# A two-layer transformer kernel on one core: projections in place of products of zeros in the first rounds, and the routing's exponential behind the first scores copy

## The chip, the cores and the metric

The kernel runs on one core of a Trainium2 chip. The metric is device time in microseconds (us) for one execution of the whole program; lower is better. Engines: PE (TensorE, matrix products), DVE (VectorE), ACT (ScalarE), POOL (GpSimd) and SP (SyncE, which issues most DMAs).

## The reference, cut to what matters

The input x has 32 sequences of 256 tokens with 128 channels, 8192 tokens in all, in float32. There are two layers of the same shape: a layer norm, an attention over the normalised tokens, a mixture of experts over the same normalised tokens whose silu is a gate, and `x = x + s * g`. Layer 0, cut to the part that the change touches:

```python
xn = _layernorm(x)                                  # per token, 128 channels
q1, k1, q2, k2 = rotary(xn @ Wq1.T), ...            # 16 heads of 8
v = xn @ Wv.T
s1, s2 = q1 @ k1.T, q2 @ k2.T                       # per head, 256 x 256
y = (causal(s1 / 8 * s2 / 8) @ v) @ Wout.T
scores = sigmoid(xn @ gate_w + bias)                # 8 experts, the best two are taken
w = top_2(scores) / (sum + 1e-6)
```

No softmax stands in layer 0: the pattern is the product of two score matrices. Layer 1 has a softmax attention and experts with a capacity; the change doesn't touch it.

## The kernel before, in words

Every engine has a program of its own, written out by hand, and they meet at semaphores. The order of instructions in each program is the order of execution. The stages are: eight rounds of the first layer norm (about the first 65 us), the loop of layer 0's attention (192 units and a tail), layer 0's experts, a stage that ends layer 0 and normalises again, and layer 1 in a loop of 32 blocks with its experts in the middle.

**The rounds.** The 64 tiles of 128 tokens go through in eight rounds of eight tiles (k = 0 to 7). For each round DVE takes the statistics (lines 1119 to 1125, called one round ahead), POOL raises the variance to the power -0.5 (line 624), DVE makes the shift and normalises three of the eight tiles (line 1130), and ACT normalises the other five (line 843). PE turns the eight tiles with transposes into two banks of PSUM (line 1752), ACT copies these to the turned tokens `XT` (line 851), and PE multiplies them with the 8 columns of the gate (line 1760, 8 products per round, each recorded as two). ACT scales round k + 1 before it copies round k. Between the transposes and the gate's products PE has to wait for ACT's copies; there `products_of_zeros` (line 1736) puts three products of 128x128 zeros with 128x512 zeros, whose result nobody reads. Twenty more of them stand ahead of round 0. In round 7 a projection stands in that place in the kernel before already.

**Projections and rotations of block 0.** A block is one sequence, two tiles. `projection(b, x)` (lines 1438 and 1439) makes query or key x of block b twice, as it is and with swapped halves, into PSUM bank 7, and DVE's `rotate(b, x)` (lines 1142 and 1147) turns it with cosines and sines. There is one such bank, so each projection waits for the rotation of the one before. In the kernel before, projections 0, 1 and 2 of block 0 stand behind the gate's products of rounds 2, 3 and 4, the values (line 1445) behind those of round 5, projection 3 in round 7. DVE's program has rotations 0, 1 and 2 in its own rounds 5, 6 and 7: rotation 0 stands ahead of the statistics of round 7, rotation 1 behind the normalising of round 6, rotation 2 behind that of round 7.

**The head of the loop.** PE's unit u = -1 makes the first kind of scores for unit 0 (line 1470) and projection 1 of block 1. Unit 0 makes the first scores for unit 1 and the second for unit 0; it waits for ACT's copy of the first scores of unit 0 (`first_scores_copy`, line 720). ACT has the exponential of the gate's sigmoid (line 854) ahead of that copy, and it waits for DVE's addition of the bias (line 1060, semaphore `gate`), which is the first step of the generator `gate_first`. DVE takes that step at u = -1, behind rotations 0 and 1 of block 1.

The lines that matter:

```python
        if k == 7:
            projection(e, m, s, 0, 3)
        else:
            products_of_zeros(e, m, 3)
        e.wait_ge(s.xt, 2 * k + 2)
```

Of the kernel before, what the change touches and what calls it, by code (L numbers as in the profile page):

```python
# [9 lines left out]
ACT = mybir.ActivationFunctionType  # L10
# [39 lines left out]
def route_step(u):  # L50

    if u < 25:
        return 1 if u == -1 else 2 if u % 6 in (1, 3) else 0
    if u < 61:
        return {25: 1, 27: 1, 31: 1, 33: 1, 37: 2, 39: 1, 45: 1, 49: 2, 51: 1}.get(u, 0)
    return 1 if u % 6 in (1, 3) else 0
# [772 lines left out]
def scalar_program(e, m, s):  # L829
    a = m.a  # L830
    for dst, src in ((m.ident[:], a["c_ident"]), (m.small[:], a["c_small"]), (m.wgA[:, 0, :], a["g0"]),
                     (m.wgA[:, 1, :], a["g1"]), (m.bias8[:], a["bias"].partition_broadcast(P)),
                     (m.scl[:], a["us"].partition_broadcast(P))):
        e.dma_start(dst, src).then_inc(s.const, 16)
    e.wait_ge(s.const, 96)
    e.copy(m.identb[:], m.ident[:])
    e.dma_start(m.upb[:], a["up_b"].rearrange("e (p j) -> p e j", j=4)).then_inc(s.upb, 16)
    route_consts(e, m, s, m.r0)
    for k in range(9):
        if k < 8:  # L840
            e.wait_ge(s.nb, k + 1)
            for i in range(8 * k, 8 * k + 5):
                ins = e.activation(m.XN[:, i, :], m.XN[:, i, :], ACT.Identity, bias=m.nb[:, i:i + 1], scale=m.rstd[:, i:i + 1])
            ins.then_inc(s.norm_a, 1)
        if k == 8:
            value_copy(e, m, s, 0)
            query_masks(e, m, s, 0, 0, range(4))
        for g in (2 * k - 2, 2 * k - 1):
            if k >= 1:
                e.wait_ge(s.xpose, g + 1)  # L850
                e.copy(m.XT[:, g * 512:g * 512 + 512], m.PS[g % 2][:]).then_inc(s.xt, 1)
    query_masks(e, m, s, 0, 1, range(4))
    e.wait_ge(s.gate, 1)
    e.activation(m.SC[:], m.SC[:], ACT.Exp, scale=-1.0).then_inc(s.gate_exp, 1)
    for u in range(-1, NU + 4):
        v, b = u % 6, u // 6
        if v == 2 and u >= 0:
            if b + 1 < NB:
                value_copy(e, m, s, b + 1)
        if u + 1 < NU:  # L860
            first_scores_copy(e, m, s, u + 1)
        if u < 0:
            continue
        if b + 1 < NB:
            if v in (0, 1):
                query_masks(e, m, s, b + 1, 0, (2 * v, 2 * v + 1))
            if v in (3, 4):
                query_masks(e, m, s, b + 1, 1, (2 * v - 6, 2 * v - 5))
        if v == 2 and b >= 1:
            e.wait_ge(s.pv, 3 * b)  # L870
            e.copy(m.RS[:, (b - 1) * 256:b * 256], m.PS[6][:, 0:256]).then_inc(s.yt, 1)

    expert_act(e, m, s, m.x0, 0, ACT.Gelu, lambda i, j: m.UB[:, i, j:j + 1])

    e.wait_ge(s.sw, 80)
    shared_act(e, m, s, 0)
    for g in range(NG + 5):
        if 0 <= g - 5 < NG:
            end_act(e, m, s, g - 5, 1)
        if g in (NG + 1, NG + 2):  # L880
            queries_copy(e, m, s, g - NG)
        if g + 1 < NG:
            shared_act(e, m, s, g + 1)
        if g == NG + 3:
            queries_apart(e, m, s, 0, range(4))
            maximum_copy(e, m, s, 0)
        if 0 <= g - 5 < NG - 1:
            end_act(e, m, s, g - 5, 2)
        if 0 <= g - 1 < NG:
            end_act(e, m, s, g - 1, 0)  # L890
        if g == NG - 1:
            queries_copy(e, m, s, 0)
            keys_copy(e, m, s, 0)
        if g == NG:
            e.activation(m.scl[:, 1:2], m.scl[:, 0:1], ACT.Exp, scale=-1.0).then_inc(s.scl_a, 1)
            keys_apart(e, m, s, 0)
            value_pad(e, m, s, 0)
        if g == NG + 1:
            keys_copy(e, m, s, 1)
        if g == NG + 2:  # L900
            keys_apart(e, m, s, 1)
    e.wait_ge(s.scl, 1)
    for t in range(NB + 1):
        if t == 1:
            e.wait_ge(s.gate, 2)
            e.activation(m.LG[:], m.LG[:], ACT.Exp).then_inc(s.gate_exp, 1)
        if t < NB:
            exponents(e, m, s, t, 0)
        if t == 0:
            end_act(e, m, s, NG - 1, 2)  # L910
        if t + 2 < NB:
            keys_copy(e, m, s, t + 2)
            keys_apart(e, m, s, t + 2)
        if t + 1 < NB:
            value_pad(e, m, s, t + 1)
        for p in pairs_combined(t):
            e.wait_ge(s.fcomb, p + 1)
            if p >= NF:
                e.wait_ge(s.fex, p - NF + 1)
            e.activation(m.ZE[p % NF], m.ZU[p % NF], ACT.Tanh, scale=0.5).then_inc(s.ftanh, 1)  # L920
        if t + 1 < NB:
            queries_apart(e, m, s, t + 1, (0, 1))
        if t < NB:
            exponents(e, m, s, t, 1)
        if t + 1 < NB:
            queries_apart(e, m, s, t + 1, (2, 3))
            maximum_copy(e, m, s, t + 1)
        if t + 3 < NB:
            queries_copy(e, m, s, t + 3)
        if t == MOE_AFTER:  # L930
            expert_act(e, m, s, m.x1, 1, ACT.Relu, lambda i, j: m.b1s[:, i // 8, j:j + 1])
# [203 lines left out]
def rotate(e, m, s, b, x):  # L1135

    i, rt = 4 * b + x, m.RT[x % 2]
    e.wait_ge(s.proj, i + 1)
    e.wait_ge(s.w0, 32)
    if x % 2 == 0 and i >= 2:  # L1140
        e.wait_ge(s.rq, 2 * b + x // 2)
    e.tensor_tensor(rt[:], m.PS[7], m.cs[:], ALU.mult).then_inc(s.rt, 1)
    if x % 2 == 1:
        if b >= 2:
            e.wait_ge((s.sc1, s.sc2)[x // 2], 6 * (b - 1))
        e.wait_ge(s.rt, i + 1)
        e.tensor_tensor(m.KK[b % 2][:, x // 2, :], rt[:, 0:256], rt[:, 256:512], ALU.add).then_inc(s.ka, 1)
# [154 lines left out]
def vector_program(e, m, s):  # L1302
# [10 lines left out]
    for k in range(8):  # L1313
# [6 lines left out]
        if k in (5, 6, 7):  # L1320
            rotate(e, m, s, 0, k - 5)
    rotate(e, m, s, 0, 3)
    rotate(e, m, s, 1, 0)
    rotate(e, m, s, 1, 1)

    gate = gate_first(e, m, s, o)
    for u in range(-1, NU + 4):
        v, b = u % 6, u // 6
        if 0 <= u < NU:
# [95 lines left out]
def projection(e, m, s, b, x):  # L1425
    e.wait_ge(s.w0, 32)
    if x == 3:
        e.wait_ge(s.vm, b + 1)
    elif 4 * b + x >= 1:
        e.wait_ge(s.rt, 4 * b + x)  # L1430
    if x == 0 and b == ROUTED_BY[0]:
        e.wait_ge(s.cnt_row, 1)
    if x == 0 and b == ROUTED_BY[1]:
        e.wait_ge(s.total_sb, 1)
    if x == 0 and b in ROUTED_BY[2:]:
        e.wait_ge(s.low_used, ROUTED_BY.index(b) - 1)
    xt = m.XT[:, b * 256:b * 256 + 256]
    e.matmul(m.PS[7][:, 0:256], m.W0[:, 2 * x, :], xt, start=True, stop=True)
    e.matmul(m.PS[7][:, 256:512], m.W0[:, 2 * x + 1, :], xt, start=True, stop=True).then_inc(s.proj, 1)

def values(e, m, s, b):
    e.wait_ge(s.rt, 4 * b + 3)
    for c in range(2):
        i = e.matmul(m.PS[7][:, c * P:(c + 1) * P], m.XT[:, b * 256 + c * P:b * 256 + (c + 1) * P], m.W0[:, 8, :],
                     start=True, stop=True)
    i.then_inc(s.vproj, 1)
# [285 lines left out]
def products_of_zeros(e, m, n):  # L1733

    for _ in range(n):
        e.matmul(m.PS[5], m.zero[:, 0:P], m.zero[:, 0:512], start=True, stop=True)

def tensor_program(e, m, s):
    PS = m.PS  # L1740
    e.wait_ge(s.zero_ready, 1)
    products_of_zeros(e, m, 20)
    e.wait_ge(s.const, 96)
    for k in range(8):
        e.wait_ge(s.norm, k + 1)
        e.wait_ge(s.norm_a, k + 1)
        for q in range(2):
            g = 2 * k + q
            if g >= 2:
                e.wait_ge(s.xt, g - 1)  # L1750
            for j in range(4):
                i = e.transpose(PS[q][:, j * P:(j + 1) * P], m.XN[:, 4 * g + j, :], m.ident[:])
            i.then_inc(s.xpose, 1)
        if k == 7:
            projection(e, m, s, 0, 3)
        else:
            products_of_zeros(e, m, 3)
        e.wait_ge(s.xt, 2 * k + 2)
        for t in range(8 * k, 8 * k + 8):
            i = e.matmul(PS[6][:, t * E:(t + 1) * E], m.XT[:, t * P:(t + 1) * P], m.wgA[:, 0, :], start=True, stop=True)  # L1760
        if k == 7:
            i.then_inc(s.logits, 1)
        if k in (2, 3, 4):
            projection(e, m, s, 0, k - 2)
        if k == 5:
            values(e, m, s, 0)
    projection(e, m, s, 1, 0)

    for u in range(-1, NU + 4):
# [224 lines left out]
```

## Time and profile before

| what | value |
|---|---|
| median of 3 runs | 1807.51 us (1805.01 to 1809.03) |
| profiled execution, its time | 1808.82 us |
| its span, first to last instruction | 1807.6 us |
| mean granted TensorE clock over the span | 0.985 |
| PE busy | 1685.4 us, 93% of the span |
| DVE, ACT, POOL busy | 1011.3, 988.9, 769.6 us |

In rows of a timeline the first number is the start in us from the span's start, the second the length, then engine, line, operation, out<-in, shapes and the count of records; a float32 product has two records. In brackets stands the idle time ahead and what ended it. The end of a matrix product is modelled and overlaps the next, so differences of starts are the better measure.

### The profile page before, as it was taken

What the parts mean: (1) busy time and instruction counts of PE and PEld (TensorE: products, weight loads), DVE (VectorE), ACT (ScalarE), POOL (GpSimd) and SP (SyncE); (2) the same over time, 40 slices, a digit from 0 to 9 for tenths busy, and PEclk for the clock granted to TensorE, in tenths of its full rate; (3) what the DMA queues carried; (4) which work ended last, traced back from release to release, by engine and by line L of the source; (5) the groups of instructions that cost most, each with busy time, mean ns of one, the idle gap of its engine ahead of it and who ended that gap; (6) DMA issues with size and microseconds to landing.
All of it is one profiled execution on the core that took longest, in us unless ns stands there. A gap on an engine that the chain in (4) does not pass through costs nothing. (4 is left out here: it accounts for less than half of the span.)

```text
span 1807.6 us, 49638 instructions
## 1 busy us (share of the span) xinstructions
PE 1685.4 (93%) x19554; PEld 1200.3 (66%) x19554; DVE 1011.3 (56%) x2111; ACT 988.9 (55%) x1803; POOL 769.6 (43%) x828
## 2 busy tenths in 40 slices
PE   9899999999998999999999689999998999989996
PEld 5544444444445999988777456666657999976664
DVE  5488788777774222221899576454452222238886
ACT  3565666666665444444454455666654444446674
POOL 4133477777773454444012103555543555540000
PEclk9999999999999999999999799999999999999999
DMA  9900001100002777775343100111112233323331
GB/s 337 374 1 2 5 26 56 64 25 28 28 27 86 222 220 225 229 210 150 114 139 105 50 2 20 37 34 37 36 33 72 85 95 87 94 79 96 96 96 43
DMA packets 172276, 170.17 MB, mean 94 GB/s; under 512 B 20272, under 2 KB 139440, under 8 KB 169104
## 3 DMA queue, kind: packets, MB, share of 16 engines
q1 hardware_dynamic: 151296, 128.83, 23.7%
q0 software_dynamic: 16832, 34.64, 5.6%
q10 hardware_dynamic: 3920, 3.53, 0.7%
q8 instruction: 159, 2.61, 0.6%
q14 instruction: 69, 0.57, 0.1%
HBM read 97.29 MB, written 69.63 MB: 92 GB/s over the span
## 5 line engine op out<-in xcount | busy, mean ns | idle before, releaser
L550 POOL DMA_INDIRECT xd<-s_XN,s_slots x256 | 250.2, 977 | 157.9 <-issue 94.4
L720 ACT ACTIVATE s_S<-ps 128x1024 f32<-128x1024 f32 x192 | 196.7, 1024 | 187.5 <-PE ps L1470 183.5
L1337 DVE TENSOR_TENSOR s_PP<-ps,s_S 128x1024 f32<-128x1024 f32 x192 | 234.8, 1223 | 105.2 <-PE ps L1470 76.6
L1470 PE MATMUL ps<-s_QM,s_KK 32*128 32x512 f32 x1536 | 220.8, 640 | 29.5 <-issue 28.7
L784 ACT ACTIVATE s_PX<-ps,s_scl 128x1024 f32<-128x1024 f32 x128 | 135.6, 1110 | 185.7 <-PE ps L1606 185.7
L1203 DVE TENSOR_REDUCE s_RS<-ps 128x8 f32<-128x1024 f32 x128 | 150.6, 1218 | 152.2 <-PE ps L1570 141.2
L583 POOL TENSOR_SCALAR_AFFINE_SELECT s_S<-s_S 128x1024 f32<-128x1024 f32 x128 | 139.7, 1091 | 154.9 <-ACT s_S L720 154.0
L799 ACT ACTIVATE s_HH<-ps,s_LG 128x256 f32<-128x256 f32 x284 | 124.2, 473 | 147.1 <-PE ps L1664 140.8
L567 POOL DMA_INDIRECT yd<-s_Y,s_to x142 | 135.9, 957 | 149.1 <-DVE s_to L1282 109.0
L799 ACT ACTIVATE s_XN<-ps,s_b1s 128x256 f32<-128x256 f32 x256 | 113.3, 473 | 131.4 <-PE ps L1664 121.5
L567 POOL DMA_INDIRECT yd<-s_XN,s_to x128 | 122.5, 957 | 129.4 <-DVE s_to L1282 103.7
L1290 DVE TENSOR_TENSOR s_Y<-ps,s_DBt 128x256 f32<-128x256 f32 x71 | 30.1, 424 | 206.4 <-PE ps L1673 192.1
L1673 PEld LDWEIGHTS ps<-s_W,s_HH 128*128 128x128 f32 x1136 | 137.9, 192 | 3.6
L1673 PE MATMUL ps<-s_W,s_HH 128*128 128x128 f32 x1136 | 138.1, 275 | 0.0
L1664 PE MATMUL ps<-s_XG,s_W 128*128 128x256 f32 x568 | 135.8, 382 | 0.2 <-DVE s_XG L1278 0.2
L1496 PEld LDWEIGHTS ps<-s_PP,s_VM 128*32 128x32 f32 x3072 | 76.1, 109 | 84.7 <-issue 55.4
L1290 DVE TENSOR_TENSOR s_XN<-ps,s_b2s 128x256 f32<-128x256 f32 x64 | 27.2, 424 | 185.3 <-issue 168.5
L1673 PEld LDWEIGHTS ps<-s_W,s_XN 128*128 128x128 f32 x1024 | 124.3, 192 | 3.2
L1673 PE MATMUL ps<-s_W,s_XN 128*128 128x128 f32 x1024 | 124.5, 275 | 0.0
L1664 PE MATMUL ps<-s_XN,s_W 128*128 128x256 f32 x512 | 123.5, 385 | 0.2 <-issue 0.2
L1470 PEld LDWEIGHTS ps<-s_QM,s_KK 32*128 32x128 f32 x1536 | 63.5, 183 | 84.7 <-issue 81.1
L1623 PE MATMUL ps<-s_PX,s_VN 128*32 128x64 f32 x4096 | 97.3, 222 | 19.6 <-issue 8.5
(217 smaller groups left out, 3087.3 us busy)
## 6 DMA issues: line engine op xcount, KB each, us to landing
s_W<-in_up_w SPq DMA_DIRECT2D x71, 256.0 KB
s_W<-in_down_w SPq DMA_DIRECT2D x71, 256.0 KB
s_X<-xd SPq DMA_DIRECT2D x135, 132.0 KB
xd<-s_zero SPq DMA_DIRECT2D x16, 1056.0 KB, 18.1
s_YG<-yd SPq DMA_DIRECT2D x32, 256.0 KB, 3.6
s_XN<-yd SPq DMA_DIRECT2D x32, 256.0 KB, 3.9
yd<-s_zero SPq DMA_DIRECT2D x7, 1056.0 KB, 27.1
s_DBt<-in_down_b SPq DMA_DIRECT2D x71, 64.0 KB
```

The costliest lines, as they stand in the source:

```text
L550: e.indirect_dma_start(out=xd, out_offset=bass.IndirectOffsetOnAxis(ap=m.slots[:, k, i:i + 1], axis=0), in_=m.XNp[:, i, 0:C + 1], in_offse ...
L567: e.indirect_dma_start(out=x.yd, out_offset=bass.IndirectOffsetOnAxis(ap=to[:, t:t + 1], axis=0), in_=x.Y[i % 4][:, t, :], in_offset=None) ...
L583: e.affine_select(out=sel, in_=sel, pattern=[[0, 8], [1, P]], compare_op=ALU.is_ge, fill=0.0, base=0, channel_multiplier=-1).then_inc(s.ma ...
L720: e.mul(m.S1[u % 3][:], m.PA, 1.0 / 64.0).then_inc(s.ev1, 1)
L784: e.activation(m.PX[hp][:, 2 * half:2 * half + 2, :].rearrange("p r n -> p (r n)"), m.ps[:, (2 + 2 * half) * 512:(4 + 2 * half) * 512], AC ...
L799: e.activation(x.HH[i % 2][:, j, :], m.PS[j][:, 0:SL], func, bias=bias(i, j)).then_inc(s.eact, 1)
L1203: e.tensor_reduce(m.MM[b % 2][:, hf, 8 * rp:8 * rp + 8], m.ps[:, 1024 * rp:1024 * rp + 1024].rearrange("p (x n) -> p x n", x=8), AX.X, ALU ...
L1337: e.tensor_tensor(m.PP[u % 4][:], m.PB[u % 2], m.S1[u % 3][:], ALU.mult).then_inc(s.prod, 1)
L1470: return e.matmul(out, m.KK[k][32 * r:32 * r + 32, kind, kc * P:(kc + 1) * P], m.QM[k][32 * r:32 * r + 32, kind, :, qc * P:(qc + 1) * P], ...
L1623: e.matmul(P4[32 * c:32 * c + 32, qb * 64:qb * 64 + 64], m.VN[b % 2][:, qb, 4 * c + hh, :], PX[:, c, x * 256 + qb * 64:x * 256 + qb * 64 + ...
L1664: e.matmul(PS[j][:, 0:SL], W[:, 0, j * P:(j + 1) * P], x.XG[i % 2][:], start=True, stop=True).then_inc(s.eup, 1)
L1673: ins = e.matmul(PS[4 + i % 2][:, c * P:(c + 1) * P], x.HH[i % 2][:, j, c * P:(c + 1) * P], W[:, 1, j * C:(j + 1) * C], start=(j == 0), st ...
```

## The change

PE: 12 products of zeros ahead of round 0 and not 20. In the place of the three in each round stand, ahead of the gate's products: projections 0, 1, 2 of block 0 in rounds 2, 3, 4 and the values in round 5 (they stood behind the gate's products before), and one product of zeros in rounds 0, 1 and 6. Of 41 products of zeros 15 are left. ACT: the wait for the gate and the exponential stand behind the copy of unit 0's first scores. DVE: the addition of the bias stands ahead of rotations 0 and 1 of block 1, and no step of the routing at u = -1.

```diff
 def route_step(u):
     if u < 25:
-        return 1 if u == -1 else 2 if u % 6 in (1, 3) else 0
+        return 2 if u % 6 in (1, 3) else 0
...
     query_masks(e, m, s, 0, 1, range(4))
-    e.wait_ge(s.gate, 1)
-    e.activation(m.SC[:], m.SC[:], ACT.Exp, scale=-1.0).then_inc(s.gate_exp, 1)
     for u in range(-1, NU + 4):
...
         if u + 1 < NU:
             first_scores_copy(e, m, s, u + 1)
         if u < 0:
+            e.wait_ge(s.gate, 1)
+            e.activation(m.SC[:], m.SC[:], ACT.Exp, scale=-1.0).then_inc(s.gate_exp, 1)
             continue
...
     rotate(e, m, s, 0, 3)
+    gate = gate_first(e, m, s, o)
+    next(gate)
     rotate(e, m, s, 1, 0)
     rotate(e, m, s, 1, 1)
-    gate = gate_first(e, m, s, o)
...
     e.wait_ge(s.zero_ready, 1)
-    products_of_zeros(e, m, 20)
+    products_of_zeros(e, m, 12)
...
-        if k == 7:
+        if k in (2, 3, 4):
+            projection(e, m, s, 0, k - 2)
+        elif k == 5:
+            values(e, m, s, 0)
+        elif k == 7:
             projection(e, m, s, 0, 3)
         else:
-            products_of_zeros(e, m, 3)
+            products_of_zeros(e, m, 1)
         e.wait_ge(s.xt, 2 * k + 2)
         for t in range(8 * k, 8 * k + 8):
             i = e.matmul(PS[6][:, t * E:(t + 1) * E], m.XT[:, t * P:(t + 1) * P], m.wgA[:, 0, :], start=True, stop=True)
         if k == 7:
             i.then_inc(s.logits, 1)
-        if k in (2, 3, 4):
-            projection(e, m, s, 0, k - 2)
-        if k == 5:
-            values(e, m, s, 0)
     projection(e, m, s, 1, 0)
```

## Rows read from the trace of the kernel before

**Rows 1.** The page, granted clock in 40 equal slices of the span.

```profile
PEclk9999999999999999999999799999999999999999
```

**Rows 2.** Timeline of PE, 0 to 80 us: rounds and the loop's head.

```profile
2.79 19.69 PE L1736 MATMUL ps<-s_zero 128*128 128x512 f32 x40 [2.79 <-POOL s_zero L619]
22.32 1.04 PE L1752 MATMUL ps<-s_ident,s_XN 128*128 128x128 f32 x8
23.19 2.74 PE L1736 MATMUL ps<-s_zero 128*128 128x512 f32 x6
25.77 1.85 PE L1760 MATMUL ps<-s_wgA,s_XT 128*128 128x8 f32 x16
27.47 1.07 PE L1752 MATMUL ps<-s_ident,s_XN 128*128 128x128 f32 x8
...
37.84 0.68 PE L1438 MATMUL ps<-s_XT,s_W 128*128 128x256 f32 x2
...
38.79 1.04 PE L1752 MATMUL ps<-s_ident,s_XN 128*128 128x128 f32 x8
...
56.15 0.69 PE L1445 MATMUL ps<-s_W,s_XT 128*128 128x128 f32 x4
...
61.83 1.07 PE L1752 MATMUL ps<-s_ident,s_XN 128*128 128x128 f32 x8
...
63.63 1.95 PE L1760 MATMUL ps<-s_wgA,s_XT 128*128 128x8 f32 x16
...
66.47 1.13 PE L1470 MATMUL ps<-s_QM,s_KK 32*128 32x512 f32 x4
...
72.24 2.09 PE L1470 MATMUL ps<-s_QM,s_KK 32*128 32x512 f32 x8 [3.57 <-issue]
...
75.98 1.14 PE L1470 MATMUL ps<-s_QM,s_KK 32*128 32x512 f32 x8
...
78.43 1.14 PE L1470 MATMUL ps<-s_QM,s_KK 32*128 32x512 f32 x8 [0.67 <-DVE s_PP L1337]
```

**Rows 3.** Timeline of ACT, 0 to 110 us.

```profile
12.42 3.96 ACT L843 ACTIVATE s_XN<-s_XN,s_nb,s_rstd 128x128 f32<-128x128 f32 x10 [1.26 <-issue]
22.95 1.07 ACT L851 COPY s_XT<-ps 128x512 f32<-128x512 f32 x2 [6.57 <-PE ps L1752]
...
70.49 0.63 ACT L854 ACTIVATE s_SC<-s_SC 128x512 f32<-128x512 f32 x1 [5.32 <-DVE s_SC L1060]
71.02 1.00 ACT L720 ACTIVATE s_S<-ps 128x1024 f32<-128x1024 f32 x1
```

**Rows 4.** Timeline of DVE, 0 to 110 us.

```profile
26.29 0.85 DVE L1130 TENSOR_SCALAR s_XN<-s_XN,s_mv,s_rstd 128x128 f32<-128x128 f32 x3
38.99 0.69 DVE L1142 TENSOR_TENSOR s_RT<-ps,s_cs 128x512 f32<-128x512 f32 x1 [11.85 <-PE ps L1439]
...
41.96 0.85 DVE L1130 TENSOR_SCALAR s_XN<-s_XN,s_mv,s_rstd 128x128 f32<-128x128 f32 x3
...
69.77 0.68 DVE L1060 TENSOR_TENSOR s_SC<-ps,s_bias 128x512 f32<-128x512 f32 x1
```

**Rows 5.** Timeline of SP: issue of the rotations' table.

```profile
17.10 0.47 SPq L496 DMA_DIRECT2D s_cs<-in_c_cs  x1
```

**Rows 6.** Its line alone: issue to landing.

```profile
DMA to landing us min/median/max: 5.8/5.8/5.8
```

**Rows 7.** Stretches: PE, PEld, DVE, ACT, POOL busy; PE's clock; DMA share; GB/s.

```profile
48.00:52.00 4.00, 4.00 (x31) 3.61 (x30) 0.69 (x1) 0.89 (x3) 0.04 (x1) 1.00 1.02 425
...
68.00:72.00 4.00, 0.66 (x4) 0.23 (x2) 1.72 (x3) 1.51 (x2) 0.49 (x2) 1.00 1.00 414
72.00:76.00 4.00, 3.76 (x15) 1.74 (x15) 1.22 (x1) 1.66 (x4) 1.64 (x2) 0.57 1.03 429
...
1031.00:1034.00 3.00, 1.79 (x17) 1.65 (x16) 0.00 (x0) 2.19 (x3) 0.00 (x0) 1.00 0.00 0
1035.00:1038.00 3.00, 3.00 (x22) 1.08 (x22) 0.30 (x1) 2.74 (x5) 0.96 (x2) 0.50 0.00 0
...
1014.00:1017.00 3.00, 3.00 (x26) 1.66 (x10) 1.20 (x2) 0.00 (x0) 0.00 (x0) 0.50 0.00 0
```

**Rows 8.** Timeline of PE around 1031 us.

```profile
1031.79 0.96 PE L1729 MATMUL ps<-s_wgA,s_XT 128*128 128x8 f32 x8
```

## The prediction

> **What bounds the kernel now.** I read the clock's slices first: full speed almost throughout, with one dip in the middle of the span [rows 1]. So the rest of the kernel gives the change nothing to repair, and only the first 80 us have to be followed. Next I read PE's timeline of that stretch [rows 2]. From the end of the opening zeros (22.32) to the first scores (66.47) PE has no gap: one group starts where the last ends. ACT and DVE wait for PE: ACT waited 6.57 us for the first transposes [rows 3], DVE 11.85 for the first projection [rows 4]. PE sets the end of the rounds, and a good part of what it does there is zeros. Behind the rounds stands one gap, 3.57 us ahead of unit 0 [rows 2]. The loop behind it follows from its own head and starts earlier if that does. The zero-filling of the DRAM buffers, which holds the DMA engines in these stretches (share 1.02 [rows 7]), isn't needed until the routing, much later, so a head start isn't taken back there.
>
> **Part 1, twelve zeros and not twenty.** One product of zeros takes (25.77 - 23.19) / 3 = 0.86 us [rows 2]; the twenty took 22.32 - 2.79 = 19.53, which is 20 x 0.86 = 17.2 and 2.3 more at the slow start. The eight that go are fast ones: 6.9 us, so round 0 starts at 15.4. Who is late next? ACT has scaled rounds 0 and 1 by 12.42 + 3.96 = 16.4 [rows 3], and copies round 0 only then, 1.07 us, to 17.5. The gate's products follow at once, so PE waits some 0.3 us in round 0 where it had no wait.
>
> **Part 2, the rounds.** A round before is transposes 0.87 (22.32 to 23.19), three zeros 2.58, the gate's products 1.70 (25.77 to 27.47): 5.15; a projection behind it adds 0.95 (37.84 to 38.79) [rows 2]. What floor is left? Round 7 has the new form already: its gate's products start 1.80 after its transposes (61.83, 63.63), since the copies start 0.63 after them and take 1.07 [rows 2, 3]. 1.80 + 1.70 = 3.50 for a round. Zeros, projection (0.95) and values (at most 0.69) fit beside the copies and cost nothing; if ACT's copies were quicker, the projection would be the bound 0.02 us later. ACT needs 1.07 and five scalings, 3.96 / 2 = 1.98, together 3.05 per round, and stays under 3.50. Followed from 15.4: round 0 ends 17.5 + 1.70 = 19.2, rounds 1 and 2 at 22.7 and 26.2.
>
> Round 3 has a new wait. Projection 1 now stands ahead of the gate's products and waits for rotation 0, which DVE has behind the normalising that ends 26.29 + 0.85 = 27.1 [rows 4]. Rotation 0.69: 27.8; transposes are done at 27.1, so PE waits 0.7, and behind it the gate's products and all later rounds. 27.8 + 0.95 + 1.70 = 30.4. Projection 2 in round 4 waits for rotation 1; from the start of rotation 0 to the end of the next normalising DVE took 42.81 - 38.99 = 3.82 [rows 4], so 27.1 + 3.8 + 0.69 = 31.6, against transposes done at 31.3: another 0.3, end 34.3. Round 5 waits for the copies, not for DVE: 37.8. Rounds 6 and 7: 41.3, 44.8. Before, the last gate's product ended at 63.63 + 1.80 = 65.4. At full clock this is 20.6 us. The rotations' table lands at 17.10 + 5.8 = 22.9 [rows 5, 6], ahead of projection 0 at 23.6: no cost, with little to spare.
>
> **Part 3, the head.** ACT's exponential ended the wait for DVE's bias (69.77 + 0.68) and its copy followed at 71.02; PE went on at 72.24 [rows 2 to 4]. Now the copy follows the first scores (66.47 + 1.13 = 67.6): 67.7 to 68.7, PE on at 68.9, and 3.3 us go. The exponential (0.63) then stands behind this copy and ahead of unit 1's, which waits a whole unit for PE anyway. The bias addition (0.68) stands on DVE ahead of rotation 0 of block 1, while PE makes the projection (0.95) for that rotation: hidden; if it isn't, up to 0.7 is lost. Two units ran slow behind the gap: unit 0 to 1 took 3.74, the next 2.45 [rows 2], with the clock at 0.57 in 72 to 76 [rows 7]. Without the gap 1.3 us go. At full clock the sum is 20.6 + 3.3 + 1.3 = 25.2.
>
> **What the zeros were for.** The price that no row gives directly is the clock's. Where it fell, rows show two kinds of work ahead of the fall: none at all (68 to 72, busy 0.66 of 4.00, all at its beginning), and thin work: in 1031 to 1034 PE did the gate's 8-column products and little else, and 1035 to 1038 ran at 0.50, after no gap longer than 1.2 us [rows 7, 8]. It stayed up over 48 to 52, which holds gate's products, a projection and transposes [rows 7]. The new rounds are made of those three, once each, so the regular ones look safe. Rounds 3, 4 and 5 don't: 1.7 us of gate's products, transposes, a wait of 0.3 to 0.7 or only the values, and gate's products again. That is nearer to the row of 1031. And the clock doesn't come back soon in thin work: 1014 to 1017 was busy for 3.00 of 3.00 and stayed at 0.50 [rows 7]. A round at 1.2 GHz takes about 6.9: twice 0.87, 0.95 and 1.70 (the half clock's price is seen in 2.09 against 1.14 for the same eight score records [rows 2]), 3.4 more than 3.50. The bounds for all rounds: nothing if the clock holds, 8 x 3.4 = 27 if it falls at once.
>
> I take a fall in round 3, 4 or 5 and no return until the dense work at the loop's head, as the nearest row is that of 1031: four rounds, 13.6, less about 1.2 for waits that a slower PE hides (0.7, 0.3 and parts). 25.2 - 12.4 = 12.8. **The sum:** against the profiled execution 1808.8 - 12.8 = 1796.0; its time stands 1.3 over the median, so 1794.7 against 1807.5, taken as 1795.
>
> **The rivals.** *The clock holds.* Then 25.2 stands: 1807.5 - 25.2 = 1782. For it: 48 to 52, and no new wait over 0.7 us. Against it: the fall behind 1031 to 1034, where there was no long gap either. The Trainium skill, "TensorE: Matmul & The Clock Gate", section "Why this matters for your kernels", has idle gaps between bursts of matmuls as what brings the clock down; by it this rival would be right. The same page, Part 1, says that the throttled state is the default and activity releases it, which speaks against taking zeros away; the trace bears out both, at 68 and at 1031.
>
> *It falls before round 3.* Round 0 has a wait of 0.3 too, and the fall may come there; then nearly all eight rounds run at 1.2 GHz: 25.2 + 1.2 - 27 leaves the time where it was, 1807. The place of the first fall may differ between runs; their times would then lie far apart.
>
> *Slower.* As the last, and the clock stays down in the loop too: PE was at half clock across 1014 to 1017 though busy throughout. Each unit costs 3.74 and not 2.45, 1.3 more; from the third such unit on the kernel is slower than before, with five it is at 1807.5 + 6 = 1813. Against it: in the kernel before, unit 0 at half clock was enough to bring it back [rows 2, 7].
>
> *It doesn't do what it says:* the wait for the copies might have been hidden by the zeros only in name. But PE had no gap there, so whatever of zeros goes must show, unless the clock takes it.
>
> **How the numbers follow.** Forecast 0.45, clock holds 0.28, early fall 0.20, slower 0.05, rest 0.02. A measurement of this kernel tells about 0.2%, 3.6 us. Faster by more: the first two, and a fifth of the early fall, 0.77. Within: 0.18. Slower: 0.05. The range has 1781 (clock holds, 1 us of hidden costs better) as its low end and 1807 (early fall) as its high one. The forecast's own range is 1789 (two rounds slow) to 1801 (six).
>
> **What would show it.** Right: round 0's transposes near 15.4; rounds 1 and 2 of 3.5; 0.7 ahead of projection 1 in round 3; then rounds of nearly 7 with the clock at 0.50; the first scores 45 to 60; no gap over 0.5 ahead of unit 0; units of 2.4 from the second on; the rest of the trace the same and shifted. Wrong: clock 1.00 through all rounds (the first rival), a dip in rounds 0 or 1 (the second), a gap ahead of unit 0 that ends with DVE or POOL, or a later stage that takes the head start back.

## The result and the profile after

| | before | changed |
|---|---|---|
| median (lowest to highest) of 20 runs each | 1803.32 us (1796.53 to 1809.03) | 1786.74 us (1772.48 to 1799.71) |
| profiled execution, its time | 1808.82 | 1787.63 |
| its span | 1807.6 | 1786.3 |
| mean granted clock over the span | 0.985 | 0.980 |
| fastest and slowest run | 12.5 us apart | 27.2 us apart |

The ratio of the runs is 0.9897, 95% interval 0.9877 to 0.9917, so the kernel became 18.6 us faster (0.0103 x 1803.3; 15 to 22 by the interval). The ratio, here and below, leaves out runs more than 1.5% above the fastest of their kernel (one of the changed kernel's twenty, 1799.71 us; one of e8_change_again, 1807.61; one of e10_early_round5, 1811.31), while the medians have them all; by the medians the gain is 16.6. Either way it is clear of 0.2%. Two things in the table ask for an explanation: the profiled execution has a lower mean clock than before although the kernel is faster, and the runs spread twice as far.

PE's timeline of the changed kernel, 0 to 60 us, answers to [rows 2]:

```profile
2.79 12.27 PE L1737 MATMUL ps<-s_zero 128*128 128x512 f32 x24 [2.79 <-POOL s_zero L619]
14.89 1.04 PE L1753 MATMUL ps<-s_ident,s_XN 128*128 128x128 f32 x8
...
18.64 1.07 PE L1753 MATMUL ps<-s_ident,s_XN 128*128 128x128 f32 x8
...
22.25 1.07 PE L1753 MATMUL ps<-s_ident,s_XN 128*128 128x128 f32 x8
...
25.86 1.07 PE L1753 MATMUL ps<-s_ident,s_XN 128*128 128x128 f32 x8
27.81 0.67 PE L1439 MATMUL ps<-s_XT,s_W 128*128 128x256 f32 x2 [0.88 <-DVE s_RT L1142]
...
30.74 1.95 PE L1753 MATMUL ps<-s_ident,s_XN 128*128 128x128 f32 x8
...
33.88 1.85 PE L1765 MATMUL ps<-s_wgA,s_XT 128*128 128x8 f32 x16
35.58 1.07 PE L1753 MATMUL ps<-s_ident,s_XN 128*128 128x128 f32 x8
...
37.38 1.95 PE L1765 MATMUL ps<-s_wgA,s_XT 128*128 128x8 f32 x16 [0.28 <-ACT s_XT L851]
...
41.52 3.42 PE L1765 MATMUL ps<-s_wgA,s_XT 128*128 128x8 f32 x16
44.79 1.95 PE L1753 MATMUL ps<-s_ident,s_XN 128*128 128x128 f32 x8
...
48.23 3.42 PE L1765 MATMUL ps<-s_wgA,s_XT 128*128 128x8 f32 x16
...
53.49 2.08 PE L1471 MATMUL ps<-s_QM,s_KK 32*128 32x512 f32 x4
...
57.51 2.09 PE L1471 MATMUL ps<-s_QM,s_KK 32*128 32x512 f32 x8
```

Round 0 starts at 14.89, round 1 at 18.64, rounds 2 and 3 follow every 3.61 us (22.25, 25.86), and in round 3 PE waits 0.88 us for DVE's rotation. Up to here all is as at full speed. Then the same work takes twice as long: eight transposes 1.95 and not 1.07 at 30.74 and 44.79, sixteen records of the gate's products 3.42 and not 1.95 at 41.52 and 48.23. The gap ahead of unit 0 is gone (no bracket at 57.51; it was 3.57 us). Stretches of the same execution (columns as in [rows 7]):

```profile
28.00:30.00 2.00, 2.00 (x16) 1.90 (x16) 1.97 (x18) 1.52 (x4) 0.04 (x1) 1.00 0.96 393
30.00:34.00 4.00, 4.00 (x20) 3.77 (x20) 3.22 (x10) 1.86 (x5) 2.43 (x2) 0.57 1.04 429
34.00:40.00 6.00, 5.72 (x53) 5.53 (x52) 0.69 (x1) 4.37 (x12) 0.72 (x1) 1.00 0.99 411
41.00:44.00 3.00, 3.00 (x14) 2.75 (x13) 0.00 (x0) 1.80 (x5) 0.00 (x0) 0.50 0.99 410
44.00:52.00 8.00, 8.00 (x34) 7.63 (x34) 1.42 (x3) 2.77 (x6) 0.00 (x0) 0.50 1.02 420
52.00:60.00 8.00, 8.00 (x21) 3.35 (x20) 2.50 (x5) 1.90 (x3) 2.23 (x3) 0.50 1.01 418
61.00:68.00 7.00, 6.16 (x66) 3.00 (x64) 6.03 (x8) 4.32 (x8) 1.56 (x2) 1.00 1.01 421
```

The granted clock is the third number from the end of each row. It fell first at the end of round 3, behind its wait, and came back within the row of 30 to 34, in the middle of round 4: the gate's products of that round at 33.88 and the transposes at 35.58 ran at full speed again. It fell again behind round 5, the one with only the values, while PE worked on round 6, and stood at 0.50 (1.2 GHz) in the rows from 41 to 60, with PE busy for the whole of them.

Where did the time come from? A unit of the loop is a good ruler. The start of unit 3's scores is 80.84 before and 66.06 after: 14.8 us. From there to the first transposes of layer 0's experts it takes 573.61 - 80.84 = 492.8 before and 558.86 - 66.06 = 492.8 after:

```profile
80.84 1.14 PE L1470 MATMUL ps<-s_QM,s_KK 32*128 32x512 f32 x8 [0.21 <-issue]
...
573.61 0.81 PE L1655 MATMUL ps<-s_ident,s_X 128*128 128x128 f32 x4 [0.49 <-ACT s_RS L871]
```

```profile
66.06 1.14 PE L1471 MATMUL ps<-s_QM,s_KK 32*128 32x512 f32 x8 [0.21 <-issue]
...
558.86 0.83 PE L1656 MATMUL ps<-s_ident,s_X 128*128 128x128 f32 x4 [0.49 <-ACT s_RS L871]
```

(The first of these fences is the kernel before, the second the changed one, both PE's timeline.) So the head start is carried whole through the attention loop. The other 6.5 of the 21.3 us between the two spans came in stages that the change doesn't touch: from the experts' first transposes to the counts of layer 1's routing it took 492.2 before and 488.8 after, and the end of layer 1, behind its experts' first transposes, gave 3.1. In the profiled executions of the experiments below the first of these lay between 488.8 and 493.7. All that follows unit 3 took 1726.8 us before (1807.6 - 80.84) and 1720.2 in the changed kernel, and between 1721.1 (e5_one_more) and 1731.3 (e6_rotate_early) in the experiments. Such differences of up to 10 us come with the execution and the chip, and nothing here ties them to the change. For the parts I therefore use unit 3 of the profiled execution and the medians of the runs.

### The profile page after: what moved, and what is told of

It is laid out like the page before. It is cut to its first block and busy times, and to the rows that moved or that the text cites. A ratio compares the mean times of both kernels' runs of the same rounds, so it can differ in the third digit from the quotient of the medians.

```text
span 1786.3 us, 49534 instructions
## 1 busy us (share of the span) xinstructions
PE 1670.2 (93%) x19502; PEld 1195.6 (67%) x19502; DVE 1011.8 (57%) x2111; ACT 989.8 (55%) x1803; POOL 771.7 (43%) x828
## 5 line engine op out<-in xcount | busy, mean ns | idle before, releaser
L1290 DVE TENSOR_TENSOR s_XN<-ps,s_b2s 128x256 f32<-128x256 f32 x64 | 27.2, 425 | 185.2 <-issue 168.5
```

## The experiments

Twelve more sets of runs were made, in four groups, each on one chip with its own runs of the kernel before; e8_change_again is the changed kernel once more, and e12_filled_again repeats e7_early_filled. The median of the kernel before there was 1809 to 1813 us, higher than the 1803 of the first chip, so only differences within a group count. The table collects them; "unit 3" is the start of its scores in the one profiled execution, "clock" the mean granted clock of that execution over 10 to 80 us, the time is the median, and the gain is worked out from the ratio and its interval. With so few runs the ratio and the medians can lie several us apart: for e8_change_again the medians give 9.2 and the ratio 14.7.

| kernel | clock | unit 3 | median (range), runs | before | gain, us |
|---|---|---|---|---|---|
| before, first profile | 0.98 | 80.84 | | | |
| changed, first profile | 0.83 | 66.06 | 1786.74 (1772 to 1800), 20 | 1803.32 | 18.6 (15 to 22) |
| e1_head | 1.00 | 75.78 | 1804.84 (1801 to 1809), 12 | 1809.20 | 3.8 (1 to 6) |
| e2_open12 | 0.95 | 74.67 | 1801.60 (1797 to 1809), 12 | 1809.20 | 7.1 (5 to 9) |
| e3_rounds | 0.93 | 68.44 | 1794.01 (1788 to 1805), 7 | 1809.20 | 13.7 (9 to 19) |
| e4_no_zeros | 0.80 | 66.78 | 1793.40 (1785 to 1804), 6 | 1809.20 | 15.4 (10 to 21) |
| e8_change_again | 0.71 | 73.64 | 1800.92 (1781 to 1808), 9 | 1810.14 | 14.7 (9 to 20) |
| e5_one_more | 1.00 | 61.04 | 1786.31 (1782 to 1791), 5 | 1810.14 | 23.0 (19 to 27) |
| e6_rotate_early | 0.85 | 64.07 | 1796.20 (1790 to 1802), 6 | 1810.14 | 13.6 (9 to 18) |
| e7_early_filled | 1.00 | 56.40 | 1782.22 (1782 to 1786), 4 | 1810.14 | 26.8 (23 to 30) |
| e9_late_filled | 0.98 | 57.88 | 1783.68 (1779 to 1784), 5 | 1812.38 | 30.4 (26 to 35) |
| e10_early_round5 | 1.00 | 55.22 | 1786.13 (1781 to 1811), 6 | 1812.38 | 26.5 (21 to 31) |
| e11_ten_opening | 0.98 | 57.32 | 1783.54 (1780 to 1794), 6 | 1812.38 | 25.0 (20 to 30) |
| e12_filled_again | 1.00 | 56.21 | 1783.22 (1780 to 1786), 5 | 1812.56 | 29.0 (25 to 33) |

**The parts alone.** e1_head takes the head's part only (ACT, DVE, `route_step`), e2_open12 the opening zeros, e3_rounds the rounds:

```diff
# e1_head, against before: of the change's diff the hunks of route_step, ACT and DVE, so
+            e.wait_ge(s.gate, 1)
+            e.activation(m.SC[:], m.SC[:], ACT.Exp, scale=-1.0).then_inc(s.gate_exp, 1)
             continue
# e2_open12, against before
-    products_of_zeros(e, m, 20)
+    products_of_zeros(e, m, 12)
# e3_rounds, against before: of the change's diff PE's hunk of the rounds, so
-        if k == 7:
+        if k in (2, 3, 4):
+            projection(e, m, s, 0, k - 2)
...
-            products_of_zeros(e, m, 3)
+            products_of_zeros(e, m, 1)
```

> The kernel before with the loop's head alone changed (ACT's exponential behind the first scores copy, DVE's bias addition ahead of rotations 0 and 1 of block 1). Theory (the parts add, the clock takes part of the rounds' gain): the gap of 3.57 us ahead of unit 0 closes to about 0.2 and the slow unit behind it goes, 4.6 us faster than before, with a spread between runs as that of before. Rival (the head start is lost behind another wait of DVE or POOL): under 2 us faster.

> The kernel before with 12 opening products of zeros in place of 20 alone. Theory: 6.9 us faster, round 0 at 15, the clock 1.00 through all rounds, as three zeros still stand in each. Rival (the opening zeros cover ACT's and DVE's first rounds): PE waits in rounds 0 to 2 and less than 4 us are left.

> The kernel before with the rounds' part alone (one product of zeros in rounds 0, 1 and 6, projections and values in place of zeros in the others; 20 opening zeros stay, the head too). PE starts round 0 at 22, so rotation 0 is early and rounds 3 and 4 have no wait for DVE; only round 5 with the values is thin. Theory (the clock falls where a round is thin or waits): sum of the part at full clock 15; the fall comes in round 5 or later, in fewer of the runs, so the median is 8 to 14 us faster. Rival (the clock falls in any round with a single product of zeros, wait or no wait): 0 to 5 us faster.

e1_head: PE's timeline shows the gap closed and the units even.

```profile
66.14 1.13 PE L1471 MATMUL ps<-s_QM,s_KK 32*128 32x512 f32 x4
...
68.55 1.14 PE L1471 MATMUL ps<-s_QM,s_KK 32*128 32x512 f32 x8 [0.22 <-issue]
...
70.96 1.14 PE L1471 MATMUL ps<-s_QM,s_KK 32*128 32x512 f32 x8 [0.21 <-issue]
```

From the first scores to unit 0 it takes 2.41 and not 5.77, to unit 1 another 2.41 and not 3.74. Unit 3 comes 5.1 us earlier, of which 0.3 is an earlier start of round 0 (21.99 for 22.32): 4.7 against the 4.6 expected; the runs give 3.8 (1 to 6). The rival, a new wait of DVE or POOL, falls.

e2_open12: round 0 starts at 14.91, 7.4 us earlier, and the clock stayed at 1.00 through the rounds. The runs give 7.1, as expected. PE waits nowhere in rounds 0 to 2, so that rival falls too. Unit 3 is 6.2 earlier only: behind the gap ahead of unit 0, which is as long as before, the clock was down for one unit more in this execution (4.03 from unit 0 to unit 1, then 3.40, where it was 3.74 and 2.45).

e3_rounds: rounds of 3.61 us with no wait in round 3, since DVE is ahead. The runs give 13.7 of the 15 that the expectation had at full clock; its rival, 0 to 5 us, falls. In the profiled execution the clock fell once in the rounds, behind the values of round 5: transposes 1.56 and not 1.07, in the row behind the 0.28 of wait.

```profile
41.57 1.95 PE L1764 MATMUL ps<-s_wgA,s_XT 128*128 128x8 f32 x16 [0.28 <-ACT s_XT L851]
43.38 1.56 PE L1752 MATMUL ps<-s_ident,s_XN 128*128 128x128 f32 x8
```

The sum of the three parts is 3.8 + 7.1 + 13.7 = 24.6 us, near the 25.2 of the sum at full clock; the intervals of the three leave it open by some 6 us either way. The changed kernel reaches 18.6 on one chip and 14.7 on another, so together the parts seem to lose what each alone keeps. By these intervals the first difference is within the noise and the second just outside it; the next kernels show where it goes.

**Is it the clock, and is it the zeros?** e4_no_zeros only removes work from the changed kernel, e5_one_more only adds work:

```diff
# e4_no_zeros, against the changed kernel
         elif k == 7:
             projection(e, m, s, 0, 3)
-        else:
-            products_of_zeros(e, m, 1)
...
# e5_one_more, against the changed kernel
         else:
             products_of_zeros(e, m, 1)
+        products_of_zeros(e, m, 1)
         e.wait_ge(s.xt, 2 * k + 2)
```

> The changed kernel without the three products of zeros that are left in rounds 0, 1 and 6 (12 opening zeros stay). Theory (thin rounds bring the clock down): PE has nothing new to do and the copies set the start of the gate's products, so at full clock the time would not move; instead the clock falls in round 0 or 1 in nearly all runs and stays at 0.50 to the head: 6 to 12 us slower than the changed kernel, and a narrower spread. Rival (only idle gaps matter): same as the changed kernel within 1 us.

> The changed kernel with one more product of zeros of 512 columns in each of the eight rounds, ahead of the gate's products. Theory (the clock's falls in thin rounds take part of the gain and cause the spread): every round becomes about 0.8 us longer at full clock, 6 us in all, but the clock stays at 1.00 through the rounds in nearly all runs: 18 to 20 us faster than before, no better than the changed kernel's median, with a spread halved to that of the kernel before. Rival (the spread comes from later stages): 6 us slower than the changed kernel, spread as wide.

> The changed kernel once more, beside the next three on the same chip. Both theories: 16 to 20 us faster than before, runs spread over more than 20 us.

e5_one_more decides it. Eight products of zeros more, 0.86 us each, and the kernel is faster than the changed one on the same chip: by 14.6 us in the medians (1786.31 against 1800.92), by 8.3 in the gains from the ratios (23.0 and 14.7). Its five runs lie within 8.4 us of each other, the nine of the changed kernel within 27, and seven of those nine are slower than all five. I had expected it no better than the changed kernel's median. Its rounds take 4.33 us in place of 3.61 (round 5 3.91), and the clock is 1.00 over 10 to 80 us. The stretches of the two, e5_one_more first and e8_change_again second:

```profile
30.00:50.00 20.00, 20.00 (x139) 16.82 (x138) 4.76 (x12) 14.28 (x34) 2.99 (x3) 1.00 1.01 416
50.00:70.00 20.00, 18.02 (x148) 8.88 (x151) 16.09 (x20) 11.20 (x18) 7.99 (x9) 1.00 1.01 420
```

```profile
30.00:50.00 20.00, 20.00 (x86) 18.47 (x86) 3.78 (x10) 9.25 (x21) 3.06 (x3) 0.50 1.01 417
50.00:70.00 20.00, 20.00 (x73) 13.61 (x73) 5.54 (x8) 6.14 (x13) 3.63 (x5) 0.54 1.01 420
```

In e8_change_again the clock fell in round 3 and stayed down through unit 0: five groups of the gate's products in a row took 3.42 us or more. Unit 3 came at 73.64, 7.6 us later than in the first profile of the very same program (0.4 of it in the opening zeros), so the place of the fall makes a good part of the spread. It doesn't make all of it: the two executions are 14.7 us apart, and the other 7.1 came behind unit 3, on a chip where the kernel before was 6.8 us slower too. The twenty runs of the changed kernel fit this: the four at a mean clock of 0.988 to 0.990 took 1772 to 1777 us, the ones at 0.973 and 0.975 took 1797 and 1800. That mean is over the whole span and doesn't say in which stage the clock was down.

e4_no_zeros isn't the clean case that I expected. The clock did fall in round 1, as foreseen, behind a wait for ACT of 1.25 us in round 0:

```profile
17.18 1.95 PE L1763 MATMUL ps<-s_wgA,s_XT 128*128 128x8 f32 x16 [1.25 <-ACT s_XT L851]
18.99 1.10 PE L1753 MATMUL ps<-s_ident,s_XN 128*128 128x128 f32 x8
20.79 3.58 PE L1763 MATMUL ps<-s_wgA,s_XT 128*128 128x8 f32 x16 [0.70 <-ACT s_XT L851]
```

But it didn't stay down to the head: it came back in the middle of round 4, fell once more in round 6 behind another wait for ACT (0.73 us), and was back in round 7. The gain of 15.4 isn't told apart from the changed kernel's 18.6 or 14.7, which were taken on other chips; the 6 to 12 us slower and the narrower spread that I expected didn't show (six runs within 19 us). Whether the three zeros that the change leaves are worth anything these runs can't tell: the clock falls with them and without them.

**Which thin place is it?** e6_rotate_early takes the wait of round 3 away; e7_early_filled adds short zeros as well; e9_late_filled has the fillers and the wait; e10_early_round5 has the early rotations and the filler of round 5 alone.

```diff
# e6_rotate_early, against the changed kernel (POOL, DVE)
     for k in range(8):
+        if k == 7:
+            query_sum(e, m, s, 0, 0)
         e.wait_ge(s.var, k + 1)
...
-    query_sum(e, m, s, 0, 0)
     query_sum(e, m, s, 0, 2)
...
-        if k in (5, 6, 7):
-            rotate(e, m, s, 0, k - 5)
+        if k in (4, 5, 6):
+            rotate(e, m, s, 0, k - 4)
# e7_early_filled, on top of it (the width w is new)
+        products_of_zeros(e, m, 1, 384 if k == 5 else 128)
         e.wait_ge(s.xt, 2 * k + 2)
# e9_late_filled: the same line on the changed kernel itself
# e10_early_round5, on top of e6_rotate_early
+        if k == 5:
+            products_of_zeros(e, m, 1, 384)
         e.wait_ge(s.xt, 2 * k + 2)
```

> The changed kernel with rotations 0, 1 and 2 of block 0 one round earlier in DVE's program and the first query sum of POOL ahead of its last power, so that projection 1 finds its bank free and round 3 has no wait. Theory: 0.9 us of the wait goes by itself; beyond it the clock falls less often in round 3, but still in round 5 with its values: 2 to 5 us faster than the changed kernel in the median. Rival (the wait is not what brings the clock down): 1 us faster.

> The kernel of the early rotations with a short product of zeros more in each round: 384 columns behind the values in round 5, 128 columns in the others, which fit mostly into the wait for ACT's copies. Theory: 1 us longer at full clock, and the clock stays at 1.00 through the rounds in most runs: 23 to 25 us faster than before, spread of 12 us or less; it would be the fastest version. Rival (regular rounds with one product each fall too, whatever is added at this size): the time and spread of the changed kernel.

> The changed kernel with the short products of zeros in each round (384 columns in round 5, 128 in the others) and the rotations where the change has them, so that the wait of 0.9 us in round 3 stays. Theory (it is this wait that brings the clock down in round 3, and the fillers mend the other rounds): the clock falls in round 3 in part of the runs, 18 to 22 us faster than before with a spread of 15 us or more. Rival (only the thin rounds mattered, the wait didn't): as the kernel with early rotations and fillers, 26 to 28 us faster and narrow.

> Early rotations and the filler of 384 columns in round 5 alone. Theory (regular rounds with one product of zeros or one projection hold the clock, round 5 with its values doesn't): as fast as the kernel with fillers in all rounds, 26 to 28 us faster than before. Rival (the regular rounds are on the edge too and need the 128 columns): wider, the median 15 to 24 us faster.

e6_rotate_early: the wait is gone (transposes at 26.39, 29.99, 33.60), and in this execution round 3 brings no fall. In the runs nothing is told apart: by the ratios the gain is 13.6 us against 14.7 for the changed kernel, by the medians it is 4.7 us faster than that kernel. The fall comes behind round 5 instead, with no gap longer than 0.28 us ahead of it, and holds to the head:

```profile
35.39 1.95 PE L1766 MATMUL ps<-s_wgA,s_XT 128*128 128x8 f32 x16 [0.28 <-ACT s_XT L852]
37.20 1.07 PE L1754 MATMUL ps<-s_ident,s_XN 128*128 128x128 f32 x8
38.11 1.62 PE L1738 MATMUL ps<-s_zero 128*128 128x512 f32 x2
39.52 3.42 PE L1766 MATMUL ps<-s_wgA,s_XT 128*128 128x8 f32 x16
```

So the expected 2 to 5 us are neither shown nor refuted. With one place of two mended, the profiled execution still fell at the other. Its time of 1796.7 isn't explained by that alone: unit 3 is only 3.0 us behind that of e5_one_more, and 10.2 us more were lost behind unit 3 (1731.3 against 1721.1), where the two programs are the same.

e7_early_filled and its repetition e12_filled_again show no fall. A filler of 128 columns takes 0.22 us. The gate's products start 2.00 us behind the first transposes and not 1.80, and then take 1.70 and not 1.81, so a round takes 3.70 instead of 3.61. The wait for ACT's copies hides next to nothing of the filler in these rounds; half of its time comes back in the gate's products, for a reason that stays open. In round 5 there was a wait of 0.28 us, and a filler of 0.64 costs 0.11 there.

```profile
27.22 1.07 PE L1754 MATMUL ps<-s_ident,s_XN 128*128 128x128 f32 x8
28.13 0.60 PE L1440 MATMUL ps<-s_XT,s_W 128*128 128x256 f32 x2
...
29.00 0.38 PE L1738 MATMUL ps<-s_zero 128*128 128x128 f32 x2
29.22 1.85 PE L1767 MATMUL ps<-s_wgA,s_XT 128*128 128x8 f32 x16
30.92 1.07 PE L1754 MATMUL ps<-s_ident,s_XN 128*128 128x128 f32 x8
```

> The kernel with early rotations and fillers in all rounds once more, as its first four runs were few. Theory: 24 to 28 us faster than before, most runs within 5 us of each other. Rival (the first four runs were lucky in where the clock's changes lay): median 16 to 20 us faster and a spread over 15 us, as the changed kernel.

Together nine runs lie between 1780.0 and 1786.5, 27 and 29 us faster than before, against 15 and a spread of 27 for the changed kernel on the same chip as the first of them. That beats both kernels. It is more than the 23 to 25 that I expected, and more than the 24.4 by which unit 3 comes early in e7_early_filled; where the rest comes from stays open, and the intervals (23 to 30, 25 to 33) reach down nearly to it.

e9_late_filled, with the rotations where the change has them, was as fast (1783.68, five runs within 6 us). Its theory fails and the rival holds as far as the runs tell: with the fillers in, the order of the rotations makes no difference that they show. Its profiled execution had a short fall in round 1, behind a wait of 0.63 us for ACT in round 0, and the clock came back by itself before round 2; as DVE ran ahead meanwhile, round 3 had no wait, so that execution doesn't show the wait and the fillers together. e10_early_round5 has the earliest unit 3 of all (55.22), but its six runs fall into 1781 to 1782 (three), 1790 to 1791 (two) and 1811 (one). The mean clock of the runs goes with it: 0.982 to 0.986 in the three, 0.981 and 0.977 in the two, 0.967 in the last. The regular rounds of 3.61 us held the clock in the profiled execution, one of the three; that they didn't hold it in the slower ones is likely and not shown, as those have no trace. So the theory (26 to 28) and the rival (15 to 24 and wide) stay unsettled: the ratio gives 26.5 without the last run, the means of all runs give 23.1.

**Fewer opening zeros still.**

```diff
# e11_ten_opening, against e7_early_filled
-    products_of_zeros(e, m, 12)
+    products_of_zeros(e, m, 10)
```

> Early rotations, fillers in all rounds and 10 opening products of zeros in place of 12. Theory (PE still sets the start of round 0, ACT's first scaling ends at 14.4): 1.2 to 1.7 us faster than with 12. Rival (round 0 and 1 then wait for ACT, which scales until 16.4, and the clock falls there): up to 8 us slower than with 12, and a wider spread.

e11_ten_opening has no gain over twelve that these runs can tell (25.0 against 26.8 and 29.0). PE's first transposes waited 2.19 us for ACT's scaling and ran at 15.30, 0.9 us before those of e7_early_filled, and the clock fell right behind that wait (the zeros of round 0 took 2.34 and not 1.25) and was back before round 1. Two of its six runs are at 1794. Much of the wait belongs to this execution: ACT began to scale at 13.13, where it began at 12.40 in e7_early_filled and at 11.88 in the changed kernel. So ten zeros leave no room for a late ACT; that twelve is the best number isn't shown.

```profile
15.30 1.25 PE L1754 MATMUL ps<-s_ident,s_XN 128*128 128x128 f32 x8 [2.19 <-ACT s_XN L844]
16.35 2.34 PE L1738 MATMUL ps<-s_zero 128*128 128x512 f32 x4
```

## Why the prediction was right or wrong

*The sum at full clock, 25.2 us.* Right. Round 0 forecast at 15.4, measured 14.89; rounds 3.50, measured 3.61 (the copies end 1.80 behind the first transposes as forecast, and the gate's products in this place took 1.80, not 1.70, as the old round 7 had shown already: 63.63 to 65.43). The wait in round 3 was forecast at 0.7 and measured 0.88 and 0.52 in the two profiled executions. Of the wait of 0.3 in round 0 0.15 came (the gate's products at 16.84, 1.95 behind the transposes): ACT began to scale at 11.88 in this execution and not at 12.42. Head 4.6, measured 4.7 in the trace. The three parts alone sum to 24.6. With the clock at 1.00 unit 3 comes 24.4 us earlier than before in e7_early_filled, with its fillers, and 25.6 in e10_early_round5, with one filler and without the wait.

*The clock falls in rounds 3 to 5 and stays down to the dense work at the head.* Half right. That the clock falls in the new rounds and takes part of the gain is shown by both profiled executions of the changed kernel and by e5_one_more. The other part, "no return until the dense work at the loop's head", failed in the first of them: the clock fell at the end of round 3, came back in round 4, and fell again in round 6. The same return between thin rounds stands in e3_rounds, e4_no_zeros, e9_late_filled and e11_ten_opening; only e8_change_again went as forecast. The forecast took it from the row of 1014 to 1017, and that row isn't thin work. Most of it is 512-column scores and 256-column products:

```profile
1013.21 2.02 PE L1566 MATMUL ps<-s_K,s_QS 32*64 32x512 f32 x16 [0.61 <-ACT s_QS L728]
1015.16 1.03 PE L1570 MATMUL ps<-s_RS,s_identb 128*128 128x256 bf16 x4
1015.98 1.72 PE L1729 MATMUL ps<-s_wgA,s_XT 128*128 128x8 f32 x8
```

Nor was the row of 1031 to 1034 the nearest to the new rounds: PE was idle for 1.2 of its 3 us, and the rounds have waits of 0.28 to 0.88. The Trainium skill, page "TensorE: Matmul & The Clock Gate", section "Why this matters for your kernels", has idle gaps as what brings the clock down. That is not enough here; the fall of e6_rotate_early stands behind no gap longer than 0.28 us. What in the rounds does bring it down, and what brings it back, stays open: with fillers in every round the profiles show a fall only behind a wait for ACT (0.63 us in e9_late_filled, 2.19 in e11_ten_opening), but no run tells which property of the work decides it.

*The forecast's size.* This step failed: "four rounds, 13.6, less about 1.2", 12.4 us for the clock. Over the 20 runs the loss is 25.2 - 18.6 = 6.6 us, about half of it (8.6 by the medians). In the profiled execution it was 10.4 (unit 3 at 66.06, where 80.84 - 25.2 = 55.6 was free), and put together otherwise than I had it. Up to the last gate's products only 5.2 were lost (48.23 against 63.63 - 20.6 = 43.0): rounds 6 and 7 ran at half clock and part of round 4, not four rounds. The rest was lost behind the rounds, where I had counted nothing: the projections, first scores and unit 0 ran at half clock as well (48.23 to 66.06 is 17.8 us, 44.02 to 56.40 in e7_early_filled is 12.4). I took four rounds as certain where the trace said only that the fall may come in any of three places, and the changed kernel has no single time. On a second chip (e8_change_again) the loss is 25.2 - 14.7 = 10.5, or 16.0 by the medians. Its profiled execution, close to the median, had unit 3 18.0 us late: 12.7 in the rounds (55.73 against 43.0), so there the 12.4 was right for them, and 5.3 behind them. That the sum's gain of 12.8 lies near that chip's (9.2 to 14.7) is in part luck, since the work behind the rounds wasn't in it. From the times it looks as if many runs on the first chip kept the clock for most of the rounds and few on the second; only one execution on each has a trace.

*The starting point.* The forecast of 1795 was taken from a median of three runs, 1807.5. With 20 runs the kernel before stands at 1803.3. Counted from there 1795 says 8 us where the sum said 12.8. The measured 1786.7 lies within the range of 1781 to 1807, but nearer its fast end.

*The rivals.* The clock holds: it did in neither of the two profiled executions of the changed kernel. The fastest four of the 20 runs (1772 to 1777) have the time that it describes, 1803.3 - 25.2 = 1778 or less, but no trace. The early fall: seen in e4_no_zeros, e9_late_filled and e11_ten_opening, where it ended in round 4, before round 2 and before round 1; in the changed kernel itself no profile shows it. Slower: not seen; the clock was back by unit 1 in both profiled executions.

## What to carry to other kernels

That an engine is busy in a timeline is no promise for its clock: here the clock fell behind rounds with many 8-column products and hardly a gap. When a filler beside such work is replaced by useful work, look at the thinnest round, and at the waits that the new order makes, not at the average. A short filler (0.22 us here, of which 0.09 a round showed) can be worth several times its cost: with it in every round the clock held in both profiles of that kernel, and a round at half clock had cost 3.1 us more (6.72 for 3.61 in e8_change_again). Before a row is taken as a likeness, read in the timeline what the engine did in it. And a median of three doesn't carry a forecast of a change of 1%: that of the kernel before stood 4.2 us above its median of twenty.

## What the runs showed of the hardware that I had not expected

A PE at half clock that is busy all the time doesn't surely get its clock back. In e8_change_again it was busy for 20.00 of 20.00 us over 30 to 50 at 0.50, and the clock rose only by unit 1. In the changed kernel's first profile it fell and was back between 30 and 34 us, in round 4, with the same kinds of products. No run shows what makes the difference. It is most of why two executions of one program had unit 3 at 66.06 and 73.64.

The opening zeros don't take a fixed time either. The same twelve ended at 14.89 in one execution of the changed kernel, at 15.31 in another, and at 16.17 in e7_early_filled, though all began at 2.79. The first few are the slow ones, which looks like a clock that rises at a different moment each time; the granted clock in the rows reads 1.00 from the start, so they don't show it.
